# Maxima scores from split queries and keys: three products of rounded parts in place of one float32 product, in a two-layer attention kernel on one core

## The chip, the cores and the metric

One NeuronCore of a Trainium2 chip runs the whole program. The metric is the time of one execution in device microseconds; before and after are timed on the same chip in turn. Engines are named as in the profile: PE (TensorE matmuls), PEld (its weight loads), DVE (VectorE), ACT (ScalarE), POOL (GpSimd), SP (the queue that issues the transfers).

## The reference, cut to what matters

Input x is (32, 64, 256), the context is (32, 1601, 256). A first layer (mean of the context, self-attention over 64 tokens, experts) changes x. The second layer begins with a cross-attention of the 64 queries of each batch to its 1601 context rows, with 16 heads of 16 dimensions. This part, for each of the 32 batches, is the bulk of the work:

```
q = (layernorm(x) @ Wq.T + bq) / 4      # 64 x 256, 16 heads
k = ctx @ Wk.T + bk                     # 1601 x 256
v = ctx @ Wv.T + bv                     # 1601 x 256
p = softmax(q k^T, over the 1601 keys)  # per head
x = x + (p v) @ Wo.T + bo
```

A gated recurrent block and a quantised feed-forward block follow, per tile of 128 tokens.

## The kernel before

**Slots.** The program is a software pipeline written out by hand. Time is cut into slots (b, k): batch b = 0 to 31, eight slots k = 0 to 7 for each, with a few more ahead and behind. Each engine runs one loop over `SLOTS` and asks in every slot which pieces of work fall there. The engines meet only at semaphores, so an engine's order in a slot is the order of the code.

**What a slot holds on PE**, in this order: the scores of slot (b, k) for the softmax (`scores`, L993 and L1000); the fills "A"; the first fill of one of two PSUM banks M (`pieces(.., "first")`: a key product L780 or a value product L787, or a piece of the first layer); the fills "B" of bank X; the scores for a maximum (`maxima`, L977); in even slots the weighing with the values (`weigh`, L1021); the fills "C"; the second fills ("second": two key products in odd slots); the fills "D".

**The bank SC.** Scores and maxima share one PSUM tile, SC, of four banks. In every slot it is used twice, strictly in turn: PE writes scores, ACT takes their exponent (`exps`, L1220), PE writes the scores of a later batch (`maxima`, L977), DVE reduces these to a maximum per query (L1559), and the next slot may begin. `maxima` runs LEAD = 6 slots ahead of the scores that it serves, and takes one quarter of the keys (400 or 401 columns) for one half c of the channels: four products, one for each group of 32 rows of the array, in plain float32. They wait for `bdq` (queries laid out by block, made by POOL, L658), for the key columns that ACT has drained (L1165), for the reduction before (`max_used`) and for the exponent of this slot (`exp_ready`).

**Float32 in parts.** Keys and values are made otherwise: context rows and weights are split into a rounded part (ACT, `high_part`, L1278, at the end of a slot) and the rest (POOL, `low_part`, L634, a slot later), both in the format float32r, and three products rest x high, high x rest, high x high are added in PSUM. That is the list `PARTS`.

**The softmax of the first layer.** Each of the 16 tiles of 128 tokens passes through 14 places q of its own. In place 6 DVE takes the row maxima of its scores SA (L1440), POOL subtracts them at the end of that slot (L760); in place 7 ACT takes the exponent (L1317) and DVE sums the rows, POOL multiplies by the reciprocal at the end of that slot (L763); in place 8, second half, PE turns the result (L882).

**The tail.** After the last batch PE runs products that nobody uses while it waits (`busy`, and `busy_rows`: four lists of the three products, on 32 rows each).

## Time and profile before

| | us |
|---|---|
| median of 3 runs | 2178.13 (2175.35 to 2179.38) |
| the profiled execution, its own time | 2174.97 |
| its span, first to last instruction | 2173.2 |
| PE busy | 1977.2 (91%) |
| PE weight loads | 1596.8 (73%) |
| DVE busy | 1328.9 (61%) |
| ACT busy | 1049.6 (48%) |
| POOL busy | 613.0 (28%) |

The 256 slots with scores take nearly the whole span. Busy shares are means over the slots. A busy PE is not an engine at its peak: its products are pipelined and a later one starts before an earlier one has ended. The mean granted clock of PE is 0.982 of full speed.

### The profile page before, as it was taken

To read this page: it belongs to the slowest core of one execution; us is meant where nothing else is said; L and a number is where in the kernel's file an instruction comes from. 1 tells how busy PE (TensorE), PEld (TensorE's weight loads), DVE (VectorE), ACT (ScalarE), POOL (GpSimd) and SP (SyncE) were. 2 spreads that over 40 slices of the span, in tenths; PEclk is the share of its full clock that TensorE was granted. 3 is DMA by queue.
4 is the path that set the end of the run, shared out by engine and by line. 5 is a ranking of instruction groups with operands and counts; after the bars stand their busy time and mean duration, and the time that the engine had idled before them with its cause. 6 is when DMAs were issued, how large, how long until landed. Compare 5 with 4: busy or idle time off the path is not lost.

```text
span 2173.2 us, 72578 instructions
## 1 busy us (share of the span) xinstructions
PE 1977.2 (91%) x31813; PEld 1596.8 (73%) x31813; DVE 1328.9 (61%) x2495; ACT 1049.6 (48%) x1534; POOL 613.0 (28%) x998
## 2 busy tenths in 40 slices
PE   4788989999999999999999999999999988999887
PEld 4567777777877777777777777777777777777764
DVE  2456755856666567656656676665666666565534
ACT  2344545554455555545555555554544444434432
POOL 3222332323233232333323223332323222122201
PEclk8899999999999999999999999999999999999999
DMA  4343423433423343334233424243342321222122
GB/s 160 140 150 109 142 87 125 149 125 124 139 88 114 116 141 129 130 107 151 83 125 109 171 77 138 92 150 106 110 148 89 116 79 31 89 83 81 48 66 72
DMA packets 99255, 243.91 MB, mean 112 GB/s; under 512 B 13312, under 2 KB 19584, under 8 KB 98944
## 3 DMA queue, kind: packets, MB, share of 16 engines
q1 hardware_dynamic: 98944, 239.26, 32.5%
q8 instruction: 256, 4.19, 0.8%
q14 instruction: 55, 0.45, 0.1%
HBM read 235.94 MB, written 3.15 MB: 110 GB/s over the span
## 4 chain that ended last, share of the span: by engine, by line
PE 71%; DVE 14%; ACT 9%; issue 4%; SPq 1%; POOL 1%; DMA 1%; DVEq 0%; POOLq 0%; ACTq 0%
PE M L780 12%; PE SC L977 9%; PE M L787 9%; PE SC L1000 8%; PE O L1021 7%; ACT probT L1220 6%; PE X L827 5%; DVE mx L1559 4%; PE SC L993 3%; PE M L827 3%; PE X L1101 2%; PE M L868 2%; DVE oT L1571 1%; PE X L1088 1%; PE M L832 1%
## 5 line engine op out<-in xcount | busy, mean ns | idle before, releaser
L1559 DVE TENSOR_REDUCE mx<-SC 128x4 f32<-128x1600 f32 (+1 forms) x256 | 466.5, 1822 | 131.4 <-PE SC L977 128.2
L1220 ACT ACTIVATE probT<-SC 128x2048 f32<-128x2048 f32 (+1 forms) x256 | 398.8, 1558 | 227.2 <-PE SC L1000 226.5
L634 POOL TENSOR_TENSOR rowsT<-raw,rowsT 128x384 fp32r<-128x384 f32 (+1 forms) x256 | 277.8, 1106 | 405.0 <-ACT rowsT L1278 404.9
L787 PE MATMUL M<-wvs,rowsT 128*128 128x256 f32 x2496 | 358.3, 292 | 3.2 <-issue 1.6
L780 PE MATMUL M<-rowsT,wks 128*128 128x400 f32 (+1 forms) x1536 | 334.5, 363 | 12.0 <-DVE V L1362 7.6
L780 PEld LDWEIGHTS M<-rowsT,wks 128*128 128x128 f32 x1536 | 276.2, 192 | 84.5 <-issue 61.5
L1362 DVE TENSOR_TENSOR V<-M,bv 128x256 f32<-128x256 f32 (+1 forms) x448 | 159.6, 398 | 287.4 <-PE M L787 276.6
L787 PEld LDWEIGHTS M<-wvs,rowsT 128*128 128x128 f32 x2496 | 314.8, 192 | 23.5 <-issue 3.5
L1165 ACT ACTIVATE kT<-M,bk 128x400 f32<-128x400 f32 (+1 forms) x256 | 151.6, 594 | 350.6 <-PE M L780 350.2
L977 PE MATMUL SC<-kT,bdq 32*128 32x400 f32 (+1 forms) x2048 | 248.1, 553 | 49.9 <-ACT probT L1220 42.7
L1021 PEld LDWEIGHTS O<-probT,V 128*17 128x17 f32 x13312 | 191.3, 98 | 72.2 <-issue 66.6
L1000 PE MATMUL SC<-bdq,kT 32*128 32x128 f32 x6656 | 235.0, 273 | 0.6 <-issue 0.3
L1000 PEld LDWEIGHTS SC<-bdq,kT 32*128 32x128 f32 x6656 | 223.1, 185 | 4.9 <-issue 1.4
L1021 PE MATMUL O<-probT,V 128*17 128x64 f32 x13312 | 215.1, 221 | 6.7 <-issue 6.7
L977 PEld LDWEIGHTS SC<-kT,bdq 32*128 32x128 f32 x2048 | 83.6, 185 | 103.2 <-issue 89.8
L626 POOL TENSOR_SCALAR rstd<-mv 128x1 f32<-128x1 f32 x80 | 18.4, 230 | 400.6 <-DVE mv L1350 399.6
L993 PE MATMUL SC<-mT,sel 32*128 32x512 bf16 (+1 forms) x1024 | 93.7, 352 | 30.2 <-DVE mx L1559 25.6
L1278 ACT ACTIVATE rowsT<-raw 128x768 fp32r<-128x768 f32 (+1 forms) x128 | 114.7, 896 | 0.4 <-ACT PT L1192 0.3
L827 PE MATMUL X<-nT,ring 128*128 128x128 f32 x736 | 93.2, 281 | 3.5 <-ACT nT L1252 3.0
L1293 ACT ACTIVATE summed<-summed 128x1601 f32<-128x1601 f32 x60 | 92.2, 1537 | 4.8 <-DMA summed<-in_ctx_dram 4.8
L827 PEld LDWEIGHTS X<-nT,ring 128*128 128x128 f32 x736 | 89.5, 196 | 6.7 <-ACT nT L1252 4.1
L993 PEld LDWEIGHTS SC<-mT,sel 32*128 32x128 bf16 (+1 forms) x1024 | 27.1, 94 | 83.4 <-DVE mx L1559 42.3
(266 smaller groups left out, 2464.1 us busy)
## 6 DMA issues: line engine op xcount, KB each, us to landing
ring<-in_ws_dram SPq DMA_DIRECT2D x428, 256.0 KB, 4.5
raw<-in_ctx_dram SPq DMA_DIRECT2D x32, 1601.0 KB, 8.4
summed<-in_ctx_dram SPq DMA_DIRECT2D x60, 800.5 KB, 4.5
ring<-rounded_scratch SPq DMA_DIRECT2D x64, 256.0 KB, 5.4
out_dram<-x SPq DMA_DIRECT2D x16, 128.0 KB, 3.2
kT<-in_ctx_dram SPq DMA_DIRECT2D x2, 800.5 KB, 8.9
x<-in_x_dram SPq DMA_DIRECT2D x11, 128.0 KB, 2.0
rounded_scratch<-wround SPq DMA_DIRECT2D x8, 128.0 KB, 2.2
```

Of the source, the lines that this page charges most:

```text
L634: pool.tensor_tensor(rowsT[1][:, c, at], raw[:, c, at], rowsT[0][:, c, at], ALU.subtract).then_inc(low_ready, 1)
L780: mm = pe.matmul(bank[:, 0:kn + kn % 2], wks[wp][:, cc, c * P:(c + 1) * P], rowsT[xp][:, cc, k0:k0 + kn + kn % 2], start=(at == cc == 0), ...
L787: mm = pe.matmul(bank[:, (t - 2 * a) * D:(t - 2 * a + 1) * D], rowsT[xp][:, cc, t * P:(t + 1) * P], wvs[wp][:, cc, :], start=(at == cc == ...
L827: mm = pe.matmul(out_[:, m, :], w[:, c, m * P:(m + 1) * P], src[:, c, :], start=(c == 0), stop=(c == C - 1))
L977: mm = pe.matmul(SC[:, j, 0:kn], bdq[mb % 2][r, c, :, :].rearrange("p e q -> p (e q)"), keys(mb, c)[r, k0:k0 + kn], start=True, stop=True, ...
L993: pe.matmul(SC[0:w, j, 0:len(ts) * P].rearrange("p (t q) -> p t q", q=P), sel[r, 0:w], mT[b % 2][c][r, :].unsqueeze(1).to_broadcast([32, l ...
L1000: mm = pe.matmul(SC[0:w, j, n * P:(n + 1) * P], keys(b, c)[r, t * P:t * P + w], bdq[b % 2][r, c, :, :].rearrange("p e q -> p (e q)"), star ...
L1021: mm = pe.matmul(O[32 * col:32 * col + W1, og * S:(og + 1) * S], values(b, c)[0:w, t * 8 + hh, :], probT[step % 3][0:w, hh // 2, n, (hh % ...
L1165: act.activation(keys(n, c)[:, k0:k0 + kn], bank[:, 0:kn], ACT.Identity, bias=bk[:, c:c + 1]).then_inc(m_used[f % 2], 1)
L1220: act.activation(probT[step % 3][0:w, :, 0:len(ts), :].rearrange("p j t q -> p j (t q)"), SC[0:w, :, 0:len(ts) * P], ACT.Exp)\
L1362: ins = dve.tensor_tensor(values(n, cc)[:, 2 * a * 8:(2 * a + m) * 8, 0:HD].rearrange("p (t h) e -> p t h e", t=m), bank[:, 0:m * D].rearr ...
L1559: dve.tensor_reduce(mx[c][:, :, n], SC[:, :, 0:KCH[n][1]], AX.X, ALU.max).then_inc(max_used, 1)
```

## The change

The scores for the maxima are made of three products of parts, as keys are. ACT rounds the key columns of the next slot's maximum (`high_keys`, last thing but `high_part` in a slot), POOL takes the rest (`low_keys`, first thing in a slot), and POOL splits each batch's queries (`split_queries`, two halves). One buffer of each part of the keys is there, so `high_keys` waits until the maxima of its slot are done (`max_filled`). PE's `maxima` now waits for `keys_low` instead of the drained keys. POOL's two softmax operations of the first layer move from the end of slots 6 and 7 of a tile to the beginning of its slots 7 and 8. In the tail `busy_rows` goes, and `busy` of "xq" grows from 5 to 15 products. Some small tiles share memory to make room; for it the first router step waits for a store of the rounded weights.

The tail's count and the buffers:

```diff
-IDLE = {'sums': 2, 'out': 9, 'conv_in': 4, 'pw': 10, 'gru_in': 7, 'hg0': 2, 'hg1': 3, 'gow': 10, 'ff_in': 7, 'ff0': 2, 'fow': 0, 'xq': 5, 'up0': 0, 'hq': 14, 'down': 4}
+IDLE = {'sums': 2, 'out': 9, 'conv_in': 4, 'pw': 10, 'gru_in': 7, 'hg0': 2, 'hg1': 3, 'gow': 10, 'ff_in': 7, 'ff0': 2, 'fow': 0, 'xq': 15, 'up0': 0, 'hq': 14, 'down': 4}
...
+        qparts = [sp.sb(f"qparts{n}", [P, C, 2, S], F32R) for n in range(2)]
+        kparts = [sp.sb(f"kparts{n}", [P, KCH[-1][1] + 1], F32R) for n in range(2)]
```

POOL, the two new functions and the loop:

```diff
+                def split_queries(b, c):
+
+                    if not 0 <= b < B:
+                        return
+                    pool.wait_ge(bd_ready, b + 1)
+                    if b:
+                        pool.wait_ge(max_filled, STEPS * (b - 1) + NQ * (c + 1))
+                    own.go(pool.tensor_copy(qparts[0][:, c, :, :], bdq[b % 2][:, c, :, :]))
+                    pool.tensor_tensor(qparts[1][:, c, :, :], bdq[b % 2][:, c, :, :], qparts[0][:, c, :, :], ALU.subtract).then_inc(queries_split, 1)
+
+                def low_keys(b, k):
+                    s = max_step(b, k)
+                    if s is None:
+                        return
+                    mb, c, n = s // STEPS, s % STEPS // NQ, s % NQ
+                    k0, kn = KCH[n][0], KCH[n][1] + KCH[n][1] % 2
+                    pool.wait_ge(keys_high, s + 1)
+                    pool.tensor_tensor(kparts[1][:, 0:kn], keys(mb, c)[:, k0:k0 + kn], kparts[0][:, 0:kn], ALU.subtract).then_inc(keys_low, 1)
...
                 for b, k in SLOTS:
                     g = STEPS * b + k
+                    low_keys(b, k)
+                    for i, q in first_layer(b, k):
+                        if q == 7:
+                            pool.wait_ge(rowmax_ready, i + 1)
+                            pool.tensor_tensor(SAs, SAs, rowmax[:, :].unsqueeze(2).to_broadcast([P, 16, S]), ALU.subtract).then_inc(shifted0, 1)
+                        if q == 8:
+                            pool.wait_ge(rowsum_ready, i + 1)
+                            pool.tensor_tensor(SAs, SAs, rowsum[:, :].unsqueeze(2).to_broadcast([P, 16, S]), ALU.mult).then_inc(p0_ready, 1)
                     if k == (2 if b == 1 else 0) and b >= 0:
                         block_queries(b + 1)
+                        split_queries(b + 1, 0)
+                    if k == 3 and b >= -1:
+                        split_queries(b + 1, 1)
                     if k == 2 and b >= -1:
                         split_max(b, 1)
                         if b < 0:
                             block_queries(0)
+                            split_queries(0, 0)
...
-                    for i, q in first_layer(b, k):
-                        if q == 6:
-                            pool.wait_ge(rowmax_ready, i + 1)
-                            pool.tensor_tensor(SAs, SAs, rowmax[:, :].unsqueeze(2).to_broadcast([P, 16, S]), ALU.subtract).then_inc(shifted0, 1)
-                        if q == 7:
-                            pool.wait_ge(rowsum_ready, i + 1)
-                            pool.tensor_tensor(SAs, SAs, rowsum[:, :].unsqueeze(2).to_broadcast([P, 16, S]), ALU.mult).then_inc(p0_ready, 1)
```

PE, `maxima` and the tail (in `fill_x`):

```diff
                     k0, kn = KCH[n]
-                    if s % STEPS == 0:
-                        pe.wait_ge(bd_ready, mb + 1)
-                    wait_drained(pe, (mb, "key", n, c))
+                    if n == 0:
+                        pe.wait_ge(queries_split, C * mb + c + 1)
+                    pe.wait_ge(keys_low, s + 1)
                     if s:
                         pe.wait_ge(max_used, s)
                     if b >= 0:
                         pe.wait_ge(exp_ready, STEPS * b + k + 1)
-                    for j in range(4):
-                        r = slice(32 * j, 32 * j + 32)
-                        mm = pe.matmul(SC[:, j, 0:kn], bdq[mb % 2][r, c, :, :].rearrange("p e q -> p (e q)"),
-                                       keys(mb, c)[r, k0:k0 + kn], start=True, stop=True, skip_group_check=True)
+                    kn += kn % 2
+                    for at, (wp, xp) in enumerate(PARTS):
+                        for j in range(4):
+                            r = slice(32 * j, 32 * j + 32)
+                            mm = pe.matmul(SC[:, j, 0:kn], qparts[wp][r, c, :, :].rearrange("p e q -> p (e q)"),
+                                           kparts[xp][r, 0:kn], start=(at == 0), stop=(at == len(PARTS) - 1), skip_group_check=True)
                     mm.then_inc(max_filled, 1)
...
                     if b >= B and n in (NT - 1, B - 1):
                         busy(IDLE.get(kind, 0))
-                        if kind == "xq":
-                            busy_rows(400)
-                            busy_rows(400)
-                            busy_rows(128)
-                            busy_rows(128)
```

ACT, the new function and the end of a slot:

```diff
+                def high_keys(b, k):
+
+                    s = max_step(b, k + 1)
+                    if s is None:
+                        return
+                    mb, c, n = s // STEPS, s % STEPS // NQ, s % NQ
+                    k0, kn = KCH[n][0], KCH[n][1] + KCH[n][1] % 2
+                    wait_drained(act, (mb, "key", n, c))
+                    if s:
+                        act.wait_ge(max_filled, s)
+                    else:
+                        act.wait_ge(cleared, 1)
+                    act.activation(kparts[0][:, 0:kn], keys(mb, c)[:, k0:k0 + kn], ACT.Copy).then_inc(keys_high, 1)
...
                     for what in x_fills(b, k, "D"):
                         drain_x(what)
+                    high_keys(b, k)
                     for n, piece in splits(b, k, 0):
                         high_part(n, piece)
```

PE's order in the middle of the program, around slot (17, 0), before. A product in plain float32 stands once here and twice in the trace:

```order
L993 MATMUL SC<-mT_0,sel 128x512 x4
L1000 MATMUL SC<-bdq,kT 128x128 x16
L787 MATMUL M<-wvs,rowsT 128x256 x12
L1088 MATMUL X<-nT,ring 128x128 x4
L977 MATMUL SC<-kT,bdq 128x400 x4
L1021 MATMUL O<-probT,V 17x64 x40
```

And in the changed kernel:

```order
L1026 MATMUL SC<-mT_0,sel 128x512 x4
L1033 MATMUL SC<-bdq,kT 128x128 x16
L818 MATMUL M<-wvs,rowsT 128x256 x12
L1109 MATMUL X<-nT,ring 128x128 x4
L1010 MATMUL SC<-kparts,qparts 128x400 x12
L1054 MATMUL O<-probT,V 17x64 x40
```

Nothing moved on PE; four products became twelve, in the same place.

ACT's order from the end of slot (16, 7) to that of slot (17, 0), before (L1165 drains keys, L1257 to L1259 the gates of the second layer, L1278 is `high_part`):

```order
L1165 ACTIVATE kT<-M,bk 128x400
L1165 ACTIVATE kT<-M,bk 128x401
L1257 ACTIVATE arena<-X 128x256
L1258 ACTIVATE arena<-X 128x256
L1259 ACTIVATE arena<-X 128x256
L1278 ACTIVATE rowsT<-raw 128x2x384
L1220 ACTIVATE probT<-SC 128x2048
L1317 ACTIVATE SA<-SA 128x1024
L1257 ACTIVATE arena<-X 128x256
L1258 ACTIVATE arena<-X 128x256
L1259 ACTIVATE arena<-X 128x256
L1293 ACTIVATE summed,msum<-summed 128x1601
```

And in the changed kernel, from the gates on:

```order
L1280 ACTIVATE arena<-X 128x256
L1313 ACTIVATE kparts<-kT 128x400
L1299 ACTIVATE rowsT<-raw 128x2x384
L1241 ACTIVATE probT<-SC 128x2048
L1352 ACTIVATE SA<-SA 128x1024
```

The rounding of the keys stands between the last drain of the slot and `high_part`, ahead of the exponent of the next slot.

POOL's order over the same slots, before (L634 is `low_part`, L658 `block_queries`, L702 the gates):

```order
L634 TENSOR_TENSOR rowsT<-raw,rowsT 128x512 x2
L760 TENSOR_TENSOR SA<-SA,rowmax 128x1024
L658 TENSOR_TENSOR bdq<-qT,mask 128x256
L634 TENSOR_TENSOR rowsT<-raw,rowsT 128x384 x2
L702 TENSOR_SCALAR arena<-arena 128x256
L763 TENSOR_TENSOR SA<-SA,rowsum 128x1024
L634 TENSOR_TENSOR rowsT<-raw,rowsT 128x384 x2
```

And in the changed kernel:

```order
L640 TENSOR_TENSOR rowsT<-raw,rowsT 128x512 x2
L684 TENSOR_TENSOR kparts<-kT,kparts 128x400
L755 TENSOR_TENSOR SA<-SA,rowmax 128x1024
L664 TENSOR_TENSOR bdq<-qT,mask 128x256
L674 CAST qparts<-bdq 128x128
L675 TENSOR_TENSOR qparts<-bdq,qparts 128x128
L640 TENSOR_TENSOR rowsT<-raw,rowsT 128x384 x2
L727 TENSOR_SCALAR arena<-arena 128x256
L684 TENSOR_TENSOR kparts<-kT,kparts 128x402
L758 TENSOR_TENSOR SA<-SA,rowsum 128x1024
L640 TENSOR_TENSOR rowsT<-raw,rowsT 128x384 x2
```

Each slot now opens with `low_keys`; the two softmax operations stand behind it, and the split of the queries ahead of `low_part`.

## Rows read from the trace of the kernel before

**Rows 1.** The page: busy time and share of the span, instructions

```profile
PE 1977.2 (91%) x31813; PEld 1596.8 (73%) x31813; DVE 1328.9 (61%) x2495; ACT 1049.6 (48%) x1534; POOL 613.0 (28%) x998
```

**Rows 2.** Chain that ended last, by engine

```profile
PE 71%; DVE 14%; ACT 9%; issue 4%; SPq 1%; POOL 1%; DMA 1%; DVEq 0%; POOLq 0%; ACTq 0%
```

**Rows 3.** Waits: engine, line, releaser: us in total, times, longest

```profile
ACT probT L1220 <- PE SC L1000: 226.5, 162, 8.8
PE SC L977 <- ACT probT L1220: 42.7, 82, 2.1
PE SC L993 <- DVE mx L1559: 25.6, 40, 1.9
ACT SA L1317 <- POOL SA L760: 9.8, 5, 4.3
```

**Rows 4.** Timeline of PE, slot (17, 0): start, length, instructions

```profile
1187.23 1.05 PE L1088 MATMUL X<-nT,ring 128*128 128x128 f32 x8
1188.21 0.95 PE L977 MATMUL SC<-kT,bdq 32*128 32x400 f32 x8
1189.09 1.31 PE L1021 MATMUL O<-probT,V 128*17 128x64 f32 x80
```

**Rows 5.** Timeline of PE where another product on 32 rows follows

```profile
1172.52 0.95 PE L977 MATMUL SC<-kT,bdq 32*128 32x400 f32 x8
1173.30 1.42 PE L868 MATMUL M<-PT 32*128 32x64 f32 x18
```

**Rows 6.** Stretches of `busy_rows` (L1044) alone: length, PE, PEld, clock, DMA

```profile
2158.00:2158.73 0.73, 0.64 (x12) 0.65 (x16) 1.00 0.05 17
2158.00:2159.28 1.28, 1.19 (x24) 1.20 (x28) 1.00 0.03 10
```

**Rows 7.** Groups by line and shape, ACT: busy us, mean ns, idle before

```profile
L1165 ACT ACTIVATE kT<-M,bk 128x400 f32<-128x400 f32 x192 | 114.1, 594 | 333.5 <-PE M L780 333.0
L1278 ACT ACTIVATE rowsT<-raw 128x768 fp32r<-128x768 f32 x96 | 81.0, 844 | 0.4 <-ACT PT L1192 0.3
L1278 ACT ACTIVATE rowsT<-raw 128x1024 fp32r<-128x1024 f32 x32 | 33.6, 1051 | 0.0
```

**Rows 8.** Timeline of ACT, end of slot (16, 7) and slot (17, 0)

```profile
1185.13 0.39 ACT L1259 ACTIVATE arena<-X 128x256 f32<-128x256 f32 x1
1185.39 0.86 ACT L1278 ACTIVATE rowsT<-raw 128x768 fp32r<-128x768 f32 x1
1186.13 1.90 ACT L1220 ACTIVATE probT<-SC 128x2048 f32<-128x2048 f32 x1
1187.89 1.08 ACT L1317 ACTIVATE SA<-SA 128x1024 f32<-128x1024 f32 x1
```

**Rows 9.** Groups by line and shape, POOL

```profile
L634 POOL TENSOR_TENSOR rowsT<-raw,rowsT 128x384 fp32r<-128x384 f32 x192 | 196.6, 1045 | 320.4 <-ACT rowsT L1278 320.3
L634 POOL TENSOR_TENSOR rowsT<-raw,rowsT 128x512 fp32r<-128x512 f32 x64 | 81.2, 1290 | 84.6 <-ACT rowsT L1278 84.6
L658 POOL TENSOR_TENSOR bdq<-qT,mask 128x256 f32<-128x256 f32 x32 | 19.8, 618 | 9.8 <-ACT qT L1242 9.2 <-PE SC L1000 0.6
```

**Rows 10.** Timeline of POOL, slot (17, 0), and of PE at L882

```profile
1184.36 1.90 POOL L760 TENSOR_TENSOR SA<-SA,rowmax 128x1024 f32<-128x1024 f32 x1 [7.33 <-DVE rowmax L1440]
...
1197.67 0.60 PE L882 MATMUL M<-ident,SA 128*128 128x128 f32 x4
```

**Rows 11.** DVE by line: duration ns min/median/max, first and last start

```profile
L1559 DVE TENSOR_REDUCE mx<-SC x256: 1792/1826/1831, 80.3 to 2079.4; 128x4 f32<-128x1600 f32 x128
L1346 DVE TENSOR_SCALAR n<-x,mv,rstd x48: 382/408/1396, 4.5 to 1668.7; 128x256 f32<-128x256 f32 x48
L1346 DVE TENSOR_SCALAR first<-x,mv,rstd x16: 401/414/1994, 254.1 to 2127.3; 128x256 f32<-128x256 f32 x16
L1572 DVE TENSOR_TENSOR oT<-osb,oT x32: 424/553/1246, 187.1 to 2122.6; 128x256 f32<-128x256 f32 x32
```

More of the change, by code:

```diff
@@ L394, in program @@
         wfac, whalf = sp.sb("wfac", [P, 2]), sp.sb("whalf", [P, 4])
[L395 removed]
+        passing = [sp.sb(f"passing{n}", [P, 256]) for n in range(2)]
+        wround = [w.bitcast(BF16) for w in passing]
         xab, bv0, bo0 = sp.sb("xab", [P, D]), sp.sb("bv0", [P, D]), sp.sb("bo0", [P, D])
         wg, bq0, bk0, bqm = sp.sb("wg", [P, C, E]), sp.sb("bq0", [P, C]), sp.sb("bk0", [P, C]), sp.sb("bqm", [P, C, 2])
[L400 removed]
+        dist, slopes = passing[0][:, 0:S], sp.sb("slopes", [P, 8])
         alibi = sp.sb("alibi", [P, 2, 4, S])
@@ L556, in _ @@
                                (bq0, d["l0bq"]), (bk0, d["l0bk"]), (dist, d["dist"])):
-                    whole(t, src, early_in)
+                    sync.dma_start(t if t is dist else full(t), src).then_inc(early_in, 16)
                 head_pairs = d["slopes"].rearrange("(j a) -> a j", a=2)
@@ L1037, in busy @@
                                   start=True, stop=True, skip_group_check=True)
-                def busy_rows(columns_):
-                    for wp, xp in PARTS:
-                        for j in range(4):
-                            r = slice(32 * j, 32 * j + 32)
-                            pe.matmul(SC[:, j, 0:columns_], rowsT[wp][r, 0, 0:P], rowsT[xp][r, 1, 0:columns_], start=True, stop=True, skip_group_check=True)
                 def fill_x(what, b):
@@ L1482, in route @@
                         go(dve.tensor_tensor(pairs, pairs, spread(goff[:, :, :], 2), ALU.add))
+                        if g == 0:
+                            for sem in round_stored:
+                                dve.wait_ge(sem, 64)
                         own(dve.tensor_tensor(egt[:, :, :, :], others(bsc[:, :, :], E), spread(bsc[:, :, :], E), ALU.is_gt))
```

8 lines of the change are left out of this document (4 added, 4 removed).

## The prediction, made before the changed kernel ran

> **What bounds the kernel now.** I read the page's busy times first: PE is busy for 91% of the span, DVE for 61%, ACT for 48%, POOL for 28% [rows 1]. The chain that ended last says the same: 71% of it is PE, 14% DVE, 9% ACT, 1% POOL [rows 2]. So work taken from PE is worth nearly its time, as long as no wait grows in its place. Where waits can grow, the list of waits tells. The one bank SC is used twice in each slot, and PE waits at the maxima for the exponent in 82 slots of 256 (42.7 us), and at the scores for DVE's maxima in 40 (25.6 us) [rows 3]. Thus the ring scores, exponent, maxima, reduction is nearly as long as PE's own work, and whatever delays the exponent is paid in such slots at once. ACT in turn waited for the scores in only 162 of 256 slots [rows 3]: in the other 94 the exponent stood behind ACT's own work. 64 of these are the short slots 3 and 7, where it stands behind a copy of the maxima that PE has just made; the rest are nearly all slots k = 0, where two key drains, a piece of the second layer and `high_part` come right before it. The timeline of slot (17, 0) shows it: from 1185.13 us ACT runs without a gap, and the exponent begins as `high_part` ends [rows 8].
>
> **PE: the block itself.** Before, a maximum takes PE from 1188.21 to 1189.09, 0.88 us, in which its eight half-products run [rows 4]. Where a product on 32 rows follows, the next begins after 0.78 us [rows 5]; so about 0.10 of the 0.88 is the change back to the other division of the array. The changed block stands in the old trace already, unused, in the tail: `busy_rows(400)` is three products of parts on four groups of 32 rows, 400 columns, in the same format, at a granted clock of 1.00 [rows 6], the level of 2.4 GHz. Twelve of them, the first block, have begun by 2158.73 us, having begun at 2158.09 (0.73 less 0.64); the next twelve by 2159.28 [rows 6]. The second block took 0.55, or 0.18 a round of four; the first 0.65, or 0.10 more, for the entry. In the pipeline each block pays entry and exit: 0.55 + 0.10 + 0.10 = 0.75, or 0.74 if the exit is 0.09 as the timeline's hundredths allow. I take 0.74. The saving is 0.88 - 0.74 = 0.14 us, on PE and, since the last product also ends that much earlier, on the ring; times 256 it is **36 us**. Two ends for this: if entry and exit cost nothing more, 0.33 us, 84 us in all, but both rows of the old block show them; if adding into PSUM costs something that the tail, which doesn't add, can't show, the saving shrinks, though the key products do add. The Trainium skill (TensorEngine Tiling (Array Packing), Key Properties) says that a change of tiling mode drains the engine; rows 4 and 5 agree, with 0.10 us. The same skill (TensorE: Matmul & The Clock Gate, Back-to-back issue gap) gives columns / 2.4 GHz + 2.5 ns, by which a round would be 0.169 us and the sum 10 us better; the rows show 0.18 and I stay with them.
>
> **ACT: `high_keys`, 256 times.** 768 columns cost 844 ns and 1024 cost 1051 [rows 7], 0.81 ns a column, so 400 cost 0.55 us; the key drains of 400 columns at 594 are the bound above. ACT's busy time becomes 1050 + 140 = 1190 us, 55%. Its instructions overlap by 0.12 us in the rows (1185.39 + 0.86 against 1186.13 [rows 8]), so each delays what stands behind by some 0.45. In slots with no second key fill it lies in ACT's idle time: it starts when the maxima are done, and the scores of the next slot are some 3 us away. I walked through ACT's rows slot by slot, put 0.45 us at that place, let the gaps take it up, and let PE's own arrival at the maxima hide what it could. Behind the exponent are queued the reduction, the next scores, and the first drains of bank M. The exponent is late by 0.42 us on the mean in slots k = 0, and PE loses 0.25 there, 7.5 us in 30 slots; slots 1 to 3 add 3.5. **Loss 11 us.** Ends: 0 if the values' fill and bank X hide it all, and 94 x 0.45 = 42 us.
>
> **POOL: `low_keys`, 256 times, and the queries.** 384 columns cost 1045 ns, 512 cost 1290 [rows 9]; 400 cost 1.08 us, 276 us in all. The split of the queries is 128 instructions on 128 columns each; the nearest row is 618 ns for 256 columns [rows 9], I take 0.4, 51 us. POOL goes from 613 to 940 us, 43%. Does PE wait for it? In slot (17, 0): ACT free at 1185.52 [rows 8], rounded at about 1186.0, subtracted at 1187.2, PE wants it at 1188.21 [rows 4]: 1.0 us to spare. Over the slots the mean of that margin by my walk is 1.1 to 3.8 us, least in slots k = 2 and 3; in some 8 slots POOL, still waiting for DVE, is late, together **3 us**. At the very start the first split queries are new on the way to the first maximum: 0.8 us and a subtraction, **1.5 us**. `low_part` starts up to 2 us later but its keys are filled a slot or more later, so nothing; were that cover gone, a late piece costs its lateness once per batch.
>
> **The softmax moved.** This is what the move buys: `low_keys` no longer stands behind a wait for DVE's row maxima, at the price that the subtraction (1.90 us, from 1184.36 [rows 10]) starts after `low_keys`, at 1187.2, and ends at 1189.1, where ACT would have begun its exponent of SA at 1187.89 [rows 8]. ACT stands 0.8 to 1.3 us in a slot that is full already, and behind it are the gates and a context sum. It takes up to 1.7 us in the seven tiles whose place 7 falls in a slot k = 0 or 2, about 0.1 in the others. The multiplication then ends after PE's want of it (1197.67 [rows 10]) in six tiles, by 0.1 to 1.6 us: 6.5 us; and one exponent of the scores comes 1.5 late. **Loss 8 us.** Ends 0 and 16 x 1.7 = 27.
>
> **DVE: hindered by POOL.** An instruction of DVE with the same work takes 408 ns in the middle and up to 1396 (L1346 on n), 414 and up to 1994 (on first), 553 against a least of 424 (L1572) [rows 11], and the long ones lie under an instruction of POOL. The reductions out of PSUM don't mind: 1792 to 1831 [rows 11]. `low_keys` mostly falls under just these reductions, since it follows the maxima; but laid on the old timeline some 140 of them meet an instruction of the kind that minds. If each costs DVE 0.4 us and an eighth of it reaches the path (DVE has 14% of the chain [rows 2]), it is **7 us**. Ends: 0, and 140 x 1.0 with a third on the path, 47 us.
>
> Nothing else: fifteen products in the tail take the place of five and 1.9 us of `busy_rows`; the wait of the router is for a store long over.
>
> **Sum.** -36 + 11 + 4.5 + 8 + 7 = -5.5 us. On the profiled execution, 2174.97 us, that is 2169.5; that execution lies 3 us under the median, 2178.13, so I forecast **2172 us**, 0.3% faster. A measurement of this kernel tells some 0.2% (4 us) from no change.
>
> **The rivals.**
> First, **the losses stay hidden** (chance 0.20). The 42.7 us of waiting at the maxima [rows 3] are spread over slots of which many also have an empty place on PE later on, and a faster PE shifts all engines alike. Then most of the 36 us remain: 2142 to 2162 us. For it: ACT at 48%, POOL at 28%. Against it: rows 8.
> Second, **DVE blocked by POOL** (0.18), slower. Mechanism: 256 subtractions of 1.08 us each hold what DVE needs for operations out of SBUF, and DVE's drains of the value banks come behind them. With the other terms at -12.5 us net, it decides from 0.05 us a slot; with 0.15 us a slot, 38 us, it comes out at 2204. The long rows in rows 11 speak for it, the reductions against. The Trainium skill states this rule more sharply (SBUF — State Buffer, Who interferes with whom): DVE and GpSimd share one pair of ports under an exclusive lock, and the second fully blocks; L1346's 1994 ns against 401 agree with it.
> Third, **ACT and POOL late** (0.17), slower. The exponent is late in all the 94 slots without a wait, and the softmax costs its upper end: -36 + 42 + 27 = +33, with half of it as likely: 2182 to 2211.
> Fourth, the block doesn't get shorter (0.03), because adding into PSUM or loading twelve weights spaces the rounds: 2178 + 20.
>
> **How the numbers follow.** The forecast's own case (0.42) spans 2163 to 2181 us. Faster by over 0.2%: 0.20 and 0.28 of the 0.42, 0.48. Within 0.2%: 0.13 of the forecast's and the near edge of the rivals, 0.20. Slower: 0.32. Since cases of both signs hold much, the range for 8 in 10 is 2150 to 2198; the likeliest case's own is 2163 to 2181.
>
> **What would show it.** In the profile after: the block from its first product to the next instruction 0.74 us; the same bank free 0.14 earlier; `high_keys` about 0.55 and `low_keys` 1.08 us; the wait of the maxima for the exponent up from 42.7 to about 55 us, few waits of PE for `low_keys`; the exponent of SA waiting for POOL some 10 us more; DVE's busy time up by 20 to 60 us while its reductions stay at 1.82. I am wrong if PE's idle time grows by over 36 us, above all before the maxima or before fills that wait for DVE's drains; or if it doesn't grow at all.

## The result, and the profile after

The changed kernel takes 2184.73 us (median of 12 runs, 2179.41 to 2192.86), the kernel before 2175.85 us (12 runs, 2170.39 to 2182.22): ratio 1.0042, 95% interval [1.0027, 1.0058]. It is 9 us, 0.4%, slower; 2172 was forecast. The time lies inside the wide range (2150 to 2198) and outside the likeliest case's own (2163 to 2181). The execution that was profiled took 2182.25 us with a span of 2180.4.

The page of the changed kernel, busy times and the chain that ended last by engine, and the span with the mean granted clock (0.982 before):

```profile
PE 1956.5 (90%) x32799; PEld 1650.2 (76%) x32799; DVE 1363.1 (63%) x2495; ACT 1161.5 (53%) x1790; POOL 924.2 (42%) x1385
...
PE 62%; DVE 17%; ACT 10%; issue 7%; POOL 3%; SPq 1%; DMA 1%; ACTq 0%; POOLq 0%; DVEq 0%
```

```profile
core 0: 2180.4 us, clock 0.973
```

Against [rows 1], PE has 20.7 us less to do, and the span is 7.2 longer; so PE stands idle 28 us longer, 224 us in place of 196. In the chain PE has gone from 71% to 62% [rows 2], and DVE, ACT, POOL and issue have all gained. No engine has taken PE's place: PE still ends most of the chain, but the others end it more often than before.

The block itself came out as forecast. PE's timeline in slot (17, 0), start, length and instructions:

```profile
1189.53 0.82 PE L1010 MATMUL SC<-kparts,qparts 32*128 32x400 f32 x12 [0.30 <-ACT probT L1241]
1190.28 1.31 PE L1054 MATMUL O<-probT,V 128*17 128x64 f32 x80
```

From the first product to the next instruction 0.75 us, where [rows 4] have 0.88 and the prediction 0.74. Over all slots in which PE goes on without a gap, the median went from 0.884 to 0.751 us. Groups by line and shape of the changed kernel, busy us, mean ns and idle before: the work that was added.

```profile
L1313 ACT ACTIVATE kparts<-kT 128x400 fp32r<-128x400 f32 x192 | 102.5, 534 | 23.9 <-PE SC L1010 23.2 <-ACT PT L1213 0.3
```

```profile
L684 POOL TENSOR_TENSOR kparts<-kT,kparts 128x400 fp32r<-128x400 f32 x192 | 203.1, 1058 | 630.6 <-ACT kparts L1313 630.4
L675 POOL TENSOR_TENSOR qparts<-bdq,qparts 128x128 fp32r<-128x128 f32 x64 | 32.3, 504 | 5.2
L674 POOL CAST qparts<-bdq 128x128 fp32r<-128x128 f32 x64 | 19.3, 302 | 2.1
```

The rounding (0.55 forecast), the subtraction (1.08) and the queries' two operations (0.4 each on the mean) have the forecast lengths. The waits of the changed kernel that answer to [rows 3], and three new ones:

```profile
ACT probT L1241 <- PE SC L1033: 138.2, 131, 6.4
PE SC L1010 <- ACT probT L1241: 46.4, 86, 2.1
PE SC L1026 <- DVE mx L1598: 31.3, 44, 2.8
ACT SA L1352 <- POOL SA L755: 18.2, 14, 3.9
PEld SC L1010 <- POOL kparts L684: 18.1, 21, 2.5
PE M L811 <- DVE V L1398: 14.7, 15, 2.8
```

ACT waits for the scores in 131 slots, not 162; it has lost the slack that the prediction counted on in [rows 3]. PE waits 3.7 us longer for the exponent, 5.7 for DVE's maxima, and 14.7 in all for DVE's drain of the value bank (7.6 us before, by the same view). Each is small. Summed over all of PE's lines in that view, PE waits 11.6 us longer for POOL (4.8 to 16.4), 9.5 for DVE (84.1 to 93.6) and 5.8 for ACT (73.7 to 79.5), together 27 of the 28 us: a sum of small latenesses, of which no engine has the most part.

Why DVE is late, its own instructions show. Number of instructions and length in ns (min/median/max) of three groups of the changed kernel:

```profile
L1598 DVE TENSOR_REDUCE mx<-SC x256: 1792/1825/1833, 84.4 to 2083.5; 128x4 f32<-128x1600 f32 x128
```

```profile
L1382 DVE TENSOR_SCALAR first<-x,mv,rstd x16: 400/824/2139, 256.4 to 2134.6; 128x256 f32<-128x256 f32 x16
L1651 DVE CUSTOM_DVE_ANT_0 rb<-first x16: 424/836/1171, 257.7 to 2135.0; 128x256 f32<-128x256 f32 x16
```

The reductions out of PSUM are untouched, as in [rows 11]. The norm of `first` has gone from 414 to 824 ns at the median. Its timeline on DVE and the one of POOL at the same time say why:

```profile
1796.20 1.13 DVE L1382 TENSOR_SCALAR first<-x,mv,rstd 128x256 f32<-128x256 f32 x1 [0.77 <-POOL rstd L633]
```

```profile
1796.13 1.05 POOL L684 TENSOR_TENSOR kparts<-kT,kparts 128x400 fp32r<-128x400 f32 x1
1797.14 0.77 POOL L704 TENSOR_TENSOR x<-x,bo 128x256 f32<-128x256 f32 x1
```

POOL makes `rstd`, for which DVE waits, and its very next instruction is `low_keys`. DVE's norm begins 0.07 us later, and ends 0.15 us after the subtraction's end: 1.13 us for 0.41 us of work. This meeting is no accident: a wait of DVE for POOL starts both at once. But it isn't the rule. By a count over the trace, 87 instructions of DVE lie under a `low_keys` and last over 50 ns more than short ones of their kind in the kernel before, and only 12 of them follow a wait for POOL.

### The profile page after: what moved, and what is told of

Its sections match the earlier page's. It is cut to its first block, busy times and chain, and to the rows that moved or that the text cites. A ratio compares the mean times of both kernels' runs of the same rounds, so it can differ in the third digit from the quotient of the medians.

```text
span 2180.4 us, 75543 instructions
## 1 busy us (share of the span) xinstructions
PE 1956.5 (90%) x32799; PEld 1650.2 (76%) x32799; DVE 1363.1 (63%) x2495; ACT 1161.5 (53%) x1790; POOL 924.2 (42%) x1385
## 4 chain that ended last, share of the span: by engine, by line
PE 62%; DVE 17%; ACT 10%; issue 7%; POOL 3%; SPq 1%; DMA 1%; ACTq 0%; POOLq 0%; DVEq 0%
PE M L811 10%; PE M L818 8%; PE SC L1010 7%; PE O L1054 6%; PE SC L1033 6%; ACT probT L1241 6%; DVE mx L1598 5%; PE X L858 5%; PE M L858 2%; PE SC L1026 2%; PE X L1122 2%; PE M L899 1%; DVE oT L1610 1%; DVE V L1398 1%; PE M L863 1%
## 5 line engine op out<-in xcount | busy, mean ns | idle before, releaser
L684 POOL TENSOR_TENSOR kparts<-kT,kparts 128x400 fp32r<-128x400 f32 (+1 forms) x256 | 272.9, 1066 | 774.8 <-ACT kparts L1313 774.3
L811 PE MATMUL M<-rowsT,wks 128*128 128x400 f32 (+1 forms) x1536 | 333.8, 362 | 19.9 <-DVE V L1398 14.7
L1010 PE MATMUL SC<-kparts,qparts 32*128 32x400 f32 (+1 forms) x3072 | 214.7, 380 | 60.9 <-ACT probT L1241 46.4
L1054 PEld LDWEIGHTS O<-probT,V 128*17 128x17 f32 x13312 | 199.0, 101 | 35.6 <-issue 34.4
L1054 PE MATMUL O<-probT,V 128*17 128x64 f32 x13312 | 222.4, 225 | 2.9 <-issue 2.9
L1010 PEld LDWEIGHTS SC<-kparts,qparts 32*128 32x128 f32 x3072 | 130.5, 187 | 114.6 <-issue 84.5
L1313 ACT ACTIVATE kparts<-kT 128x400 fp32r<-128x400 f32 (+1 forms) x256 | 136.8, 534 | 40.3 <-PE SC L1010 39.3
L858 PE MATMUL X<-nT,ring 128*128 128x128 f32 x736 | 93.0, 280 | 4.0 <-ACT nT L1273 3.0
L858 PEld LDWEIGHTS X<-nT,ring 128*128 128x128 f32 x736 | 89.0, 195 | 7.4 <-ACT nT L1273 4.3
```

The source lines that it names most:

```text
L684: pool.tensor_tensor(kparts[1][:, 0:kn], keys(mb, c)[:, k0:k0 + kn], kparts[0][:, 0:kn], ALU.subtract).then_inc(keys_low, 1)
L811: mm = pe.matmul(bank[:, 0:kn + kn % 2], wks[wp][:, cc, c * P:(c + 1) * P], rowsT[xp][:, cc, k0:k0 + kn + kn % 2], start=(at == cc == 0), ...
L858: mm = pe.matmul(out_[:, m, :], w[:, c, m * P:(m + 1) * P], src[:, c, :], start=(c == 0), stop=(c == C - 1))
L1010: mm = pe.matmul(SC[:, j, 0:kn], qparts[wp][r, c, :, :].rearrange("p e q -> p (e q)"), kparts[xp][r, 0:kn], start=(at == 0), stop=(at == l ...
L1054: mm = pe.matmul(O[32 * col:32 * col + W1, og * S:(og + 1) * S], values(b, c)[0:w, t * 8 + hh, :], probT[step % 3][0:w, hh // 2, n, (hh % ...
```

## The experiments

All times are medians; each ratio is to the kernel before, run in turn on the same chip. Its median was 2174.8 us beside e1 to e8, 2176.2 beside e9 to e11, 2175.6 beside e12.

The profile leaves two readings open. Either GpSimd's subtraction holds up VectorE's instructions that lie beside it, or the new work is simply late for those who wait for it: ScalarE's rounding for the exponent, GpSimd's for the softmax and for PE. The first is theory D in the expectations. A third possibility, that the block's gain isn't real, was put to the test first.

**e1: the block alone.** The kernel before, whose block for the maxima multiplies parts of two fixed tiles, rounded once, so that the true maxima are left out:

```diff
-                        mm = pe.matmul(SC[:, j, 0:kn], bdq[mb % 2][r, c, :, :].rearrange("p e q -> p (e q)"),
-                                       keys(mb, c)[r, k0:k0 + kn], start=True, stop=True, skip_group_check=True)
+                    kn += kn % 2
+                    for at, (wp, xp) in enumerate(PARTS):
+                        for j in range(4):
+                            r = slice(32 * j, 32 * j + 32)
+                            mm = pe.matmul(SC[:, j, 0:kn], fixedq[r, :], fixedk[r, 0:kn],
+                                           start=(at == 0), stop=(at == len(PARTS) - 1), skip_group_check=True)
```

> The kernel before, with its maxima made as three products on 32 rows, but out of two fixed tiles that are rounded once at the start: no rounding and no subtraction of keys or queries, softmax where it was. (It leaves out the true maxima.) Theory P, that the block's saving is real and was given back by the other engines: the block costs PE 0.13 us less, 256 times, 33 us; less some 7 us if the weighing after it stays slower as in the changed kernel: about 2150 us, ratio to before 0.985 to 0.989. Rival Q, that a shorter block is worth little in itself because the ring of bank SC or other waits take it up: 2165 to 2176, ratio 0.995 to 1.000.

Measured: 2151.68 us, ratio 0.9894 [0.9876, 0.9911]. That is theory P: the shorter block is worth 23 us. In the groups of PE, before and in e1:

```profile
L977 PE MATMUL SC<-kT,bdq 32*128 32x400 f32 (+1 forms) x2048 | 248.1, 553 | 49.9 <-ACT probT L1220 42.7 <-DVE mx L1559 5.1 <-POOL bdq L658 1.6
L1021 PE MATMUL O<-probT,V 128*17 128x64 f32 x13312 | 215.1, 221 | 6.7 <-issue 6.7
```

```profile
L980 PE MATMUL SC<-fixedk,fixedq 32*128 32x400 f32 (+1 forms) x3072 | 214.1, 379 | 50.4 <-ACT probT L1223 43.1 <-DVE mx L1564 5.2 <-POOL bdq L659 1.6
L1024 PE MATMUL O<-probT,V 128*17 128x64 f32 x13312 | 217.1, 221 | 10.3 <-issue 10.2
```

and the page of e1:

```profile
PE 1947.1 (91%) x32837; PEld 1644.2 (76%) x32837; DVE 1325.3 (62%) x2495; ACT 1051.8 (49%) x1536; POOL 614.4 (29%) x998
```

Busy time is a poor gauge of one pipelined group, since the lengths of neighbours overlap; over PE as a whole it fell by 30.1 us (256 x 0.13 = 33 by the block's timeline). Of these 30, the span gave back 22.8: 7 us turned into idle time on PE, spread over waits that each grew by less than 4 us (the two groups above by 0.5 and 3.6).

**e2, e3, e4: the two passes over the keys, one by one.** The changed kernel, where from the fifth slot on GpSimd subtracts two columns in place of 400 (e2), ScalarE rounds two columns (e3), or both (e4); these parts of the maxima's operands are left out. For e2 (e3 has the same split at L1313):

```diff
-  pool.tensor_tensor(kparts[1][:, 0:kn], keys(mb, c)[:, k0:k0 + kn], kparts[0][:, 0:kn], ALU.subtract).then_inc(keys_low, 1)
+  if s < 4:
+      pool.tensor_tensor(kparts[1][:, 0:kn], keys(mb, c)[:, k0:k0 + kn], kparts[0][:, 0:kn], ALU.subtract).then_inc(keys_low, 1)
+  else:
+      pool.tensor_tensor(kparts[1][:, 0:2], keys(mb, c)[:, k0:k0 + 2], kparts[0][:, 0:2], ALU.subtract).then_inc(keys_low, 1)
```

> The changed kernel, but POOL's subtraction takes 2 columns of the keys instead of 400 from the fifth on (the rest of the second part is left out); every wait stays. Theory D, that POOL's 273 us of subtractions hold up DVE: PE's extra waits for DVE (about 20 us) go, DVE's busy time falls by some 30 us, 2164 us, ratio to before 0.992 to 0.996. Theory A, that ACT's rounding delays the exponent: nothing but the 5 us of PE waiting for POOL goes, 2180, ratio 1.001 to 1.003.

> The changed kernel, but ACT's rounding takes 2 columns instead of 400 from the fifth on (the rest of the first part is left out); every wait stays and POOL subtracts all 400. Theory D: 2181 to 2184, ratio 1.002 to 1.004. Theory A: the exponent comes on time again, 11 us less, 2173, ratio 0.997 to 1.000.

> The changed kernel with both the rounding and the subtraction on 2 columns from the fifth on. Theories D and A together leave the waits themselves, the split of the queries and the softmax a place later: by theory D plus A 2155 us, ratio 0.990. If the losses came mostly from the order (softmax a place later, waits on POOL) and not from the work, it stays at 2170 or above, ratio 0.997 or more.

Measured: e2 2170.65 us, ratio 0.998 [0.9967, 0.9994]; e3 2184.68, 1.0054 [1.0037, 1.0072]; e4 2156.61, 0.9926 [0.991, 0.9942]. e2 fell between the two forecasts (2164 by theory D, 2180 by theory A); e3 and e4 came within 1 and 2 us of theory D's. Taken out of the changed kernel, the subtraction gives 14 us and the rounding nothing. Taken out second, the rounding gives 14 and the subtraction 28. In either order the two together cost 28. And e4 lies only 5 us above e1: the new waits, the query split, the moved softmax and the later start, everything in the change but the block and the two passes, cost 5 us together. DVE in e2, the page and the norm of `first`:

```profile
PE 1955.6 (90%) x32799; PEld 1648.9 (76%) x32799; DVE 1333.2 (61%) x2495; ACT 1162.3 (54%) x1790; POOL 704.8 (32%) x1385
```

```profile
L1385 DVE TENSOR_SCALAR first<-x,mv,rstd x16: 402/412/1991, 254.9 to 2123.7; 128x256 f32<-128x256 f32 x16
```

DVE's busy time is 30 us under that of the changed kernel, for the same 2495 instructions, and the norm is back at 412 ns. But the other sign of theory D hardly came: PE's waits for DVE, summed over all its lines, are 91.7 us in e2 against 93.6, and those for POOL 11.8 against 16.4. And with the subtraction its lateness went too, so the 14 us may hold both.

**e5: as late, but harmless.** To part "GpSimd's subtraction holds DVE up" from "GpSimd is late for those who wait for it", e2 with two powers on one column ahead of the small subtraction:

```diff
+                        for n in range(2):
+                            own.go(pool.tensor_tensor(spare[n][:, :], ones[:, 0:1], neg_half[:, :], ALU.pow))
```

> The changed kernel, where from the fifth slot on the 400-column subtraction of GpSimd is replaced by two powers on one column (0.57 us each in the trace) and a subtraction of two columns; the low parts of the keys are left out but for two columns. GpSimd is as long in use at the head of each slot as in the changed kernel (1.14 us and a little against 1.07), and its later work and TensorE's wait for the low parts come as late. Theory D (the subtraction stretches VectorE's instructions that lie under it, and a power on one column doesn't): as e2, 2168 to 2173 us. Rival L (GpSimd is late for what waits for it): as the changed kernel, 2182 to 2188 us.

Measured: 2167.53 us, ratio 0.9958 [0.9943, 0.9973]. So rival L is out, and the time is theory D's. The page, GpSimd's group of the powers, and PE's waits for the low part:

```profile
PE 1952.8 (90%) x32799; PEld 1651.4 (76%) x32799; DVE 1296.3 (60%) x2495; ACT 1161.2 (54%) x1790; POOL 980.9 (45%) x1889
```

```profile
L689 POOL TENSOR_TENSOR spare<-ones,neg_half 128x1 f32<-128x1 f32 x504 | 289.6, 575 | 756.7 <-ACT kparts L1319 736.5
```

```profile
PEld SC L1016 <- POOL kparts L690: 30.0, 32, 2.6
PE SC L1016 <- POOL kparts L690: 16.7, 23, 2.3
```

GpSimd is busy longer than in the changed kernel (980.9 us against 924.2), and PE waits for it more (30.0 us in the weight loads' view against 18.1), and yet the kernel is 17 us faster. DVE's busy time is the least of all, 1296.3 us. The same meeting as above, DVE and then POOL:

```profile
1789.36 0.41 DVE L1388 TENSOR_SCALAR first<-x,mv,rstd 128x256 f32<-128x256 f32 x1 [0.75 <-POOL rstd L634]
```

```profile
1789.29 1.35 POOL L689 TENSOR_TENSOR spare<-ones,neg_half 128x1 f32<-128x1 f32 x2
```

The norm takes 0.41 us under two powers. So lateness alone isn't what made the changed kernel slow; what GpSimd reads and writes beside DVE is. How much lateness costs, e5 doesn't show: over all its lines PE waits 30.6 us for POOL (16.4 in the changed kernel), but only 78.6 for DVE (93.6), whose busy time is 67 us under the changed kernel's and 37 under that of e2. One may hide the other. The 37 us may come from GpSimd's older passes over SBUF (`low_part`), which the powers push to other places; that wasn't tried.

**e6: the subtraction alone.** The kernel before with a subtraction of 400 columns at the head of each slot, that nobody waits for (the memory layout and the warm-up are the changed kernel's):

```diff
+                    wait_drained(pool, (mb, "key", n, c))
+                    if s:
+                        pool.wait_ge(max_filled, s)
+                    own.go(pool.tensor_tensor(kparts[1][:, 0:kn], keys(mb, c)[:, k0:k0 + kn], keys(mb, c)[:, k0:k0 + kn], ALU.subtract))
```

> The kernel before, with its float32 block for the maxima and the softmax at the old place, and one GpSimd subtraction of 400 float32 columns added at the head of each slot, whose result nobody reads or waits for; of the change it keeps the memory layout and the shorter warm-up alone. It computes what the reference does. Theory D: the subtraction costs by itself about what it gave back in e2, 14 us, so 2185 to 2192 us. Rival W (the 14 us of e2 were the new wait of TensorE for the low parts, or hung on the shorter block): 2176 to 2180 us, the warm-up's 2 to 4 us alone.

Measured: 2185.92 us, ratio 1.0055 [1.0042, 1.0069], 11 us. The page of e6, and the norm of `first`:

```profile
PE 1985.0 (91%) x31775; PEld 1601.6 (73%) x31775; DVE 1355.6 (62%) x2495; ACT 1051.2 (48%) x1534; POOL 831.9 (38%) x1257
```

```profile
L1377 DVE TENSOR_SCALAR first<-x,mv,rstd x16: 406/932/1996, 258.9 to 2138.3; 128x256 f32<-128x256 f32 x16
```

With PE's block, ACT's work and the waits as before, DVE has 26.7 us more to do than in [rows 1], again with the same instructions. Nobody waits for this subtraction, so this is the cleanest price of the stretching, though GpSimd's own later work comes later as well. The mean clock of PE, lower here (0.974 in this profile), isn't the cause: in the execution of e6 with a mean of 0.980 the span was 2183.2 us, and in the 15 of the kernel before with 0.980 it was 2170.3 to 2176.1.

**e7 and e11: the softmax at its old place.** The changed kernel with the two operations back at the end of slots q = 6 and 7 (e7), and that with the small subtraction of e2 (e11):

```diff
                 for b, k in SLOTS:
                     low_keys(b, k)
-                    for i, q in first_layer(b, k):
-                        if q == 7:
-                            pool.wait_ge(rowmax_ready, i + 1)
...
+                    for i, q in first_layer(b, k):
+                        if q == 6:
+                            pool.wait_ge(rowmax_ready, i + 1)
```

> The changed kernel with GpSimd's two softmax operations of the first layer back at the end of slots 6 and 7, where they stood before. It computes what the reference does. The prediction's step (the softmax moved costs 8 us): 2177 us. Theory D (the move costs little, since ScalarE waits for it in few slots: 18.2 us against 9.8): 2180 to 2188 us, no difference beyond 3 us. Rival: the old place is now worse, since the subtraction pushes it further back at the slot's end: 2190 us or more.

> The kernel with the softmax operations at their old place (e7), with GpSimd's subtraction on two columns from the fifth slot on; the low parts of the keys are left out but for two columns. Theory H (in e7 the low parts of the next slot stand behind GpSimd's wait for VectorE's row maxima and sums and the 1.9 us operations; the size of the subtraction is not what counts): the subtraction's 14 us come off and no more, 2218 to 2228 us. Rival (the 53 us are the subtraction meeting the softmax operations): 2170 to 2185 us.

Measured: e7 2237.39 us, ratio 1.0293 [1.0276, 1.031]; e11 2208.12, 1.0145 [1.0129, 1.0161]. I had expected next to nothing of e7 and was wrong by 53 us; only the rival's "2190 us or more" holds. e11 lies between its two forecasts. The waits in e7:

```profile
POOL SA L791 <- DVE rowmax L1476: 79.6, 14, 11.9
PEld SC L1010 <- POOL kparts L684: 67.4, 33, 5.5
POOL SA L794 <- DVE rowsum L1481: 67.1, 16, 8.3
PE SC L1010 <- POOL kparts L684: 61.0, 24, 5.3
```

At the old place POOL arrives early and waits up to 11.9 us for DVE's row maxima. In the kernel before, nothing that PE needs for the maxima of every slot was queued behind that wait. Now `low_keys` of the next slot is, and PE stands up to 5.3 us at the maxima. With the small subtraction 29 us of the 53 came off in place of the 14 that I expected, and some 37 remain over e2: the head of the queue is the larger part, and the size of the subtraction adds to it, since it comes on top of the lateness there.

**e9: the warm-up.** The changed kernel with `IDLE["xq"]` at 5 and the four calls of `busy_rows` back. These are the products that nobody uses in the tail.

> The changed kernel with the warm-up of the last expert batch as it stood before (5 fillers and four rounds of row products in place of 15 fillers). It computes what the reference does. If the warm-up makes the first scores come 4.5 us later (107.6 us against 103.1 after the span's start), the time is 2179 to 2182 us. Rival: the start differs from profile to profile by other things (102.5 to 107.6 in kernels with one and the same warm-up), then 2183 to 2187 us, no difference.

Measured: 2186.45 us, ratio 1.005 [1.0035, 1.0065]: no difference from the changed kernel. The rival holds. The condition of the expectation could not have come true: these products run only after the last exponent, near 2158 us in [rows 6], and can't move the first scores.

**e8, e10, e12: the high parts alone.** A softmax may subtract any number near the maximum, as long as exponent and sum subtract the same one. So one product of the high parts will do, and no low part is made (e8). e10 is e8 with ScalarE's rounding cut to two columns (the rest of that operand is left out); e12 is e8 with the rounding as one copy on GpSimd, at the head of the slot.

```diff
-                    low_keys(b, k)
...
-                    pe.wait_ge(keys_low, s + 1)
+                    pe.wait_ge(keys_high, s + 1)
...
-                    for at, (wp, xp) in enumerate(PARTS):
...
+                        mm = pe.matmul(SC[:, j, 0:kn], qparts[0][r, c, :, :].rearrange("p e q -> p (e q)"),
+                                       kparts[0][r, 0:kn], start=True, stop=True, skip_group_check=True)
```

and e12 against e8, in GpSimd's program and, the last line, in ScalarE's:

```diff
+                    wait_drained(pool, (mb, "key", n, c))
+                    if s:
+                        pool.wait_ge(max_filled, s)
+                    pool.tensor_copy(kparts[0][:, 0:kn], keys(mb, c)[:, k0:k0 + kn]).then_inc(keys_high, 1)
...
-                    high_keys(b, k)
```

> The changed kernel with one product of the rounded high parts for the maxima in place of three; no low parts of keys or queries are made, and TensorE waits for ScalarE's rounding. The maxima are then those of rounded scores, and the exponents subtract these. TensorE's block loses two of its three rounds of 0.18 us in each of 256 slots, at most 92 us off the 2157 us of e4; the reduction of VectorE (1.82 us, 256 times) then ends the wait more often. Theory D: 2070 to 2110 us. Rival (the block is hidden behind VectorE's reductions and the order of ScalarE once it is short): 2120 to 2150 us.

> The kernel with the product of the high parts alone, where ScalarE rounds only two columns of the keys from the fifth slot on; the rest of the maxima's operand is left out. Theory A (ScalarE's rounding delays the exponent once nothing slower stands beside it, as e2 against e4 gave 14 us): 2096 to 2108 us. Rival (the rounding is hidden, as after against e3 gave nothing): 2114 to 2120 us.

> The kernel with the product of the high parts alone (e8), where GpSimd makes the high part of the keys, at the head of the slot, as one copy, in place of ScalarE. It computes what the reference does. ScalarE gets back the 13 us of e8 against e10. Theory D (GpSimd's long passes stretch VectorE's instructions, whatever their operation): 11 us of that are given back, as in e6, and TensorE now waits for GpSimd at the head of the slot: 2112 to 2125 us. Rival (a copy is short enough on GpSimd and hinders less than a subtraction): 2100 to 2110 us.

Measured: e8 2117.83 us, ratio 0.9746 [0.9725, 0.9767], between its two forecasts (up to 2110, from 2120); e10 2104.64, 0.9678 [0.9661, 0.9695]; e12 2104.11, 0.9673 [0.9644, 0.9702]. ACT's rounding again costs 13 us where no subtraction stands beside it. Put on GpSimd it costs nothing on balance: the rival of e12 held, theory D's 11 us did not come. GpSimd's copy, and the norm of `first` in e12:

```profile
L685 POOL CAST kparts<-kT 128x400 fp32r<-128x400 f32 x192 | 101.8, 530 | 352.0 <-ACT kT L1186 270.7 <-PE SC L1010 80.8
```

```profile
L1381 DVE TENSOR_SCALAR first<-x,mv,rstd x16: 402/588/1987, 245.4 to 2056.1; 128x256 f32<-128x256 f32 x16
```

The copy takes 530 ns where the subtraction takes 1058, and has one input, not two. It does stretch DVE's norm somewhat (588 ns at the median), and it also spares ACT the small instruction that e10 kept, 28 us of ACT's busy time; whether its length, its single input or that relief makes it cheap, no run parts. e12 computes what the reference does and is the fastest, 3.3% under the kernel before and 3.7% under the changed one.

## Why the prediction was wrong

The forecast was 5.5 us faster on the profiled execution; it is 9 slower. The runs let the sum be read off in three parts:

```
                                               predicted   measured
block shorter (e1 - before)                      -36         -23
all but block and passes (e4 - e1)               +12.5        +5
passes over the keys, ACT and POOL (after - e4)  +18         +28
sum                                               -5.5       +10
```

The last line is 10 and not 9 because the kernel before was timed again beside the runs.

**The first step that failed is "work taken from PE is worth nearly its time".** The term's size on PE was right: 0.13 us a slot for 0.14. But 23 of 36 us came out in e1, 7 us were lost to waits that grew, none of them by 4 us, and the rest did not come off PE's busy time (30 against 36). The chain gives PE 71%, not 100 [rows 2]: 71% of 33 us is 23, an agreement that one kernel does not prove and that no run here tests. I priced DVE's loss at its share of the path and the gain at its full length.

**The granted clock of PE was put at nothing, without a reason.** Its mean over the span fell from 0.982 to 0.979 in e1 and 0.973 in the changed kernel. The clock stands at one of two levels, 1.2 or 2.4 GHz; worked out from these means and the spans, the time at the lower one is about 78, 90 and 118 us (an estimate). The changed kernel runs e1's block and, but for a few in the tail, the same other products, and yet PE is busy 9.4 us longer than in e1 (1956.5 against 1947.1), nearly a third of the 30 us between their spans. From one execution to the next of the kernel before the span follows the clock too: 2176.8 and 2176.9 us at a mean of 0.975, 2165.7 at 0.985, some 1.1 us for each thousandth. Over all their executions the means are 0.980 before and 0.974 changed, which is some 6 of the 9 us if that slope holds between kernels (an estimate). At an equal 0.977 the changed kernel's spans are 2177.6 to 2181.6 us, those before 2173.2 to 2177.3. So roughly half of the loss goes with the clock. Whether the clock fell because PE waits more was not tested by itself.

**DVE hindered by POOL, 7 us, was the mis-sized loss**: 11 us by e6 (9 to 15 by its interval), and at most 14 by e2, where the lateness went as well. The mechanism, the instructions that mind and those that don't, and DVE's busy time (34 us up, 20 to 60 forecast) were right. Too low was "an eighth of it reaches the path": in e6 26.7 us of stretching cost 11, four tenths; between the changed kernel and e5 67 us are worth 17, a quarter. Why it is more than an eighth stays open: the instructions that wait for a POOL result are 12 of 87, and by which of the others the time reaches PE was not followed. This is the mechanism of the second rival, at the size from which it decides and not at its 2204 us. It named that point, 0.05 us a slot; 11 to 14 us over 256 slots is 0.043 to 0.055. Without its subtraction the kernel is 4 us faster than before (e2), with it 9 slower. The Trainium skill (SBUF — State Buffer, Who interferes with whom) says that, where VectorE runs in a mode with two ports, whoever issues first holds the pair of SBUF ports that it shares with GpSimd for the whole instruction, and the other is fully blocked. The 1.13 us norm above agrees: it ended 0.15 us after the subtraction. That the norm runs in such a mode, no run here shows.

**ACT: `high_keys`, 11 us**, is 0 or 14 us, by what stands beside it (e3 against e2 and e4; 13 in e10). The slot walk found the right size for a kernel with nothing else late. That the rounding gone gains nothing while the subtraction gone gains 14 suggests that what the subtraction delays ends last while both are there; by which engine in each slot was not followed, and stays open.

**POOL: `low_keys` late, 3 us.** PE's new waits for it are there (18.1 us in the weight loads' view, 6.0 on PE proper), but e5, with 30.0 and 16.7, lost nothing by them on balance. **The softmax moved, 8 us:** the exponent of SA waits 8.4 us more for POOL (9.8 to 18.2), where some 10 were forecast, and all the small items together cost 5. The reason given for the move, that `low_keys` must not stand behind a wait for DVE, was right and worth far more than the prediction made of it: e7 puts 53 us on it.

**The start, 1.5 us.** PE's timeline at the first maxima, before and after:

```profile
75.84 1.16 PE L827 MATMUL X<-nqT,ring 128*128 128x128 f32 x8 [0.47 <-ACT nqT L1236]
78.56 1.72 PE L977 MATMUL SC<-kT,bdq 32*128 32x400 f32 x8 [1.56 <-POOL bdq L658]
```

```profile
77.98 1.16 PE L858 MATMUL X<-nqT,ring 128*128 128x128 f32 x8 [0.47 <-ACT nqT L1257]
83.00 1.37 PE L1010 MATMUL SC<-kparts,qparts 32*128 32x400 f32 x12 [3.86 <-POOL qparts L675]
```

The first maxima begin 4.4 us later. Of this 2.3 us are the split queries, where 1.5 were forecast. The other 2.1 are there already at L858, and differ from profile to profile: with the same code up to that line it starts at 76.14 us in e9, 76.60 in e5 and 77.98 here.

**What came out as forecast:** the block, the lengths of all new instructions, the unchanged reductions, little waiting for `low_keys`, and PE's idle time up by less than 36 us (28). Of the prediction's list of what would show the forecast right, the lengths and waits were met but for the wait at the maxima (46.4 us, 55 forecast), and the sign was wrong all the same: the list checked lengths and single waits, and the loss was spread over many, and over PE's own clock.

**The other rivals.** The first, losses that stay hidden, is out by e2 to e4, and the fourth, a block that doesn't get shorter, by e1. The third, ACT and POOL late, spans 2182 to 2211 us, and the measured time lies in it by luck: by itself the rounding gives back nothing (e3), and the softmax, the waits and the split together cost 5 us, not 27.

## What to carry to other kernels

Don't price a gain on the busiest engine at its full length: here a saving of 33 us gave 23, with the engine at 71% of the chain. Its share of the chain is a first guess, from one case. A pass over SBUF on GpSimd with two inputs can be paid on VectorE: here 256 subtractions of some 1 us cost 11 to 14 us, though neither engine is the busiest. Look at the granted clock before and after as well: it can take back part of what was saved. And ask whether the number must be exact at all: against the changed kernel, dropping two of three products and the low parts gave 3.1% (e8), and 3.7% with the rounding moved to GpSimd (e12), where three cheaper products in place of the exact one lost 0.4%.

## What the hardware showed that I had not expected

What a GpSimd instruction reads and writes matters to VectorE more than how long it lasts. Under 0.57 us powers on one column, DVE's norm of 256 columns kept its 0.41 us (median 411 ns in e5, at most 454), while under subtractions of 400 columns it went to 824 ns at the median. Operation and width changed together, so which of the two counts isn't shown. The rule cited above makes no exception for narrow instructions; no row here shows a one-column power holding anything.

Two passes that cost 28 us together give back 14 and 14 in one order of removal, 0 and 28 in the other (e2 to e4). A part undone by itself, e3, would have acquitted ACT's rounding, which costs 13 us in e8.

The granted clock, as a mean over the span, went down with PE's idle time and not with its work: 0.982 before (PE idle for 196 us), 0.979 in e1 (203), 0.973 in the changed kernel (224), 0.967 in e8 (240), 0.962 in e7 (259). e6 doesn't fit (0.974 with 199). In e7 PE runs the products of the changed kernel and is busy 1975.2 us in place of 1956.5. In the changed kernel the weighing with the values, which the change does not touch, takes 222.4 us in place of the 215.1 shown with e1:

```profile
L1054 PE MATMUL O<-probT,V 128*17 128x64 f32 x13312 | 222.4, 225 | 2.9 <-issue 2.9
```

So a part of what is taken off PE can go back into its other products, here 7 us in this group. That the clock is all of it was not tested, and no run changed the clock alone.
